# Last feed-forward of a graph network: sixteen candidates by four searches of 256 columns, exponentials by pairs of tiles

## What is computed

```
input_acts = gelu(x @ input_patterns.T)                  # 256, all of them kept
process_acts = gelu(input_repr @ process_input_weights.T)  # 1250 x 1024
top_p_acts, top_p_idx = top_k(process_acts, 128)
p_weights = softmax(top_p_acts)
agg_value = einsum('bsk,bskd->bsd', p_weights, process_values[top_p_idx])
output_acts = gelu(agg_value @ output_input_weights.T)   # 256, all of them kept
out = output_acts @ output_patterns ;  x = x + out
```

## Time and profile before

| | us |
|---|---|
| median of 3 runs | 1332.99 |
| lowest and highest | 1331.43 and 1338.83 |
| span of the profiled execution | 1331.9 |
| PE busy | 1255.2 |
| DVE busy | 557.6 |
| ACT busy | 462.4 |
| POOL busy | 198.8 |

### The profile page before, as it was taken

The page is one execution under the profiler, slowest core; times in us unless marked ns, Lnnn a source line. Parts: engine busy times, 40 slices in busy tenths (PEclk is TensorE's granted clock), DMA queues, the critical chain, the costliest instruction groups (busy, mean ns, idle before and its releaser), DMA issues.

```text
span 1331.9 us, 19378 instructions
## 1 busy us (share of the span) xinstructions
PE 1255.2 (94%) x6567; PEld 828.1 (62%) x6568; DVE 557.6 (42%) x1512; ACT 462.4 (35%) x991; POOL 198.8 (15%) x201
## 2 busy tenths in 40 slices
PE   4899999999999989989999999999989999989797
PEld 2554467466546645548877887877655587664465
DVE  8999833111124335110000000001187345677894
ACT  5799643222112220001111111111113343338893
POOL 2000000000000004711111111111173000013480
PEclk8999999999999989989999999999998999999899
DMA  9200000000020020175134611662563000200011
GB/s 206 95 1 1 1 2 1 0 1 1 0 95 21 30 108 1 20 259 207 47 118 164 233 50 46 229 231 83 205 188 117 1 33 1 72 0 0 1 30 49
DMA packets 42949, 98.25 MB, mean 74 GB/s; under 512 B 4113, under 2 KB 6603, under 8 KB 41845
## 3 DMA queue, kind: packets, MB, share of 16 engines
q1 hardware_dynamic: 28613, 68.70, 15.5%
q0 software_dynamic: 6144, 16.45, 4.5%
q10 hardware_dynamic: 8112, 12.08, 2.5%
HBM read 81.02 MB, written 16.17 MB: 73 GB/s over the span
## 4 chain that ended last, share of the span: by engine, by line
PE 73%; DVE 13%; POOL 4%; issue 4%; ACT 2%; DMA 2%; ACTq 1%; DVEq 1%; POOLq 0%
PE psum L450 34%; PE psum L1864 14%; PE psum L1908 7%; PE psum L1840 4%; PE psum L2070 4%; POOL slot_tokens L711 3%; PE psum L478 1%; PE psum L1936 1%; PE psum L1887 1%; DVE sb_hT_conv L1455 1%; ACT sb_htok L834 1%; DVE sb_stats L458 1%; DVE sb_x_res L1269 1%; PE psum L1981 1%; POOL sb_blk L655 1%
## 5 line engine op out<-in xcount | busy, mean ns | idle before, releaser
L450 PEld LDWEIGHTS psum<-sb_blk,sb_w_reg 128*128 128x128 f32 x1792 | 204.0, 192 | 12.7 <-issue 12.7
L450 PE MATMUL psum<-sb_blk,sb_w_reg 128*128 128x128 f32 x1792 | 205.2, 275 | 1.6 <-issue 1.6
L1864 PE MATMUL psum<-sb_z_reg_r,sb_hT_conv_r 125*125 125x512 f32 x400 | 169.0, 423 | 0.6 <-DVE sb_z_last L1109 0.4
L450 PE MATMUL psum<-sb_w_reg,sb_hT_conv 128*125 128x512 f32 (+1 forms) x376 | 167.2, 594 | 0.0
L1239 DVE TENSOR_TENSOR sb_blk<-sb_blk,psum 128x256 f32<-128x256 f32 x56 | 23.6, 421 | 276.9 <-ACT sb_blk L805 276.9
L1864 PE MATMUL psum<-sb_htok_r,sb_hT_conv_r 125*125 125x512 f32 x300 | 118.8, 396 | 0.0
L450 PEld LDWEIGHTS psum<-sb_w_reg,sb_hT_conv 128*125 128x125 f32 (+1 forms) x376 | 68.3, 187 | 76.6 <-issue 75.9
L450 PE MATMUL psum<-sb_hT_conv,sb_w_reg 128*128 128x416 f32 (+3 forms) x336 | 101.8, 459 | 0.8 <-ACT sb_hT_conv L484 0.8
L1908 PE MATMUL psum<-sb_w_reg,sb_blk 128*128 128x512 f32 x224 | 100.8, 592 | 0.0
L784 ACT CAST sb_hT_conv_r<-sb_a_reg 125x625 fp32r<-125x625 f32 x80 | 56.2, 716 | 115.5 <-PE psum L1864 115.5
L1864 PEld LDWEIGHTS psum<-sb_z_reg_r,sb_hT_conv_r 125*125 125x125 f32 x400 | 74.7, 187 | 23.0 <-issue 5.4
(11 more groups left out here) (396 smaller groups left out, 1753.0 us busy)
## 6 DMA issues: line engine op xcount, KB each, us to landing
sb_hT_conv<-w_expert SPq DMA_DIRECT2D x7, 2048.0 KB, 9.9
sb_w_reg<-w_expert SPq DMA_DIRECT2D x6, 2048.0 KB, 18.2
sb_hT_conv<-w_expert SPq DMA_DIRECT2D x7, 1024.0 KB, 12.4
slot_outs<-sb_blk ACTq DMA_DIRECT2D x28, 256.0 KB
sb_w_reg<-w_expert SPq DMA_DIRECT2D x6, 1024.0 KB, 20.0
sb_w_reg<-w_gnn SPq DMA_DIRECT2D x1, 4096.0 KB, 44.4
sb_w_reg<-w_qkv SPq DMA_DIRECT2D x1, 3072.0 KB, 21.3
slot_outs<-sb_blk ACTq DMA_DIRECT2D x1, 2560.0 KB, 10.6
```

What stands on the lines that cost most here:

```text
L450: ins = e.matmul(out, l, r, start=(n == 0), stop=(n == len(pairs) - 1))
L1864: ins = e.matmul(psum[0:TP, b, :], counts_at(l, 2 * i + n // NT)[:, s % HALF_T, :], z[s], start=(n == 0), stop=(n == len(pairs) - 1))
```

## The change

- `rest` is searched in four quarters of 256 columns, eight values each, into a list `found` of 32; `searched` is signalled by the last of these four instead of by the second full search, and `rest` is no longer written by DVE.
- Part 1 searches the 32 for the eight largest, copies the last value of each quarter behind them (columns 32 to 35), replaces the eight in a copy of the 32 and searches that for the next eight.
- Part 3 counts over all 36 columns of `found` instead of over the sixteen candidates, and makes the flag in two instructions instead of three.
- vec_refine's last instruction becomes a tensor_scalar with three pointers.
- The exponentials have five buffers, the two new ones in w_reg, and are made for tiles 0 and 1 together, then in each odd stage for two tiles. `len(wexp)` takes the place of 3 in the code of DVE and PE.

```
-                e.max(cand[:, i, 1:9], r).then_inc(v_own, v.up())
-                e.tensor_copy(cand[:, i, 0:1], thr[:, c]).then_inc(v_own, v.up())
+                for q in range(QUARTERS):
+                    width = N_PROC // QUARTERS
+                    e.max(found[:, q * 8:(q + 1) * 8], r[:, q * width:(q + 1) * width]).then_inc(
+                        *((searched, 1) if q == QUARTERS - 1 else (v_own, v.up())))
+                e.tensor_copy(best[:, i, 0:1], thr[:, c]).then_inc(v_own, v.up())
+                e.wait_ge(searched, i + 1)
...
-                e.match_replace(r, cand[:, i, 1:9], r, REPLACED).then_inc(v_own, v.up())
+                e.max(best[:, i, 1:9], found[:, 0:CAND]).then_inc(v_own, v.up())
+                lasts = found[:, 0:CAND].rearrange("p (q n) -> p q n", n=8)[:, :, 7]
+                e.tensor_copy(found[:, CAND:], lasts).then_inc(v_own, v.up())
                 e.wait_ge(v_own, v.n)
+                e.match_replace(others, best[:, i, 1:9], found[:, 0:CAND], REPLACED).then_inc(v_own, v.up())
+                e.wait_ge(v_own, v.n)
+                e.max(best[:, i, 9:17], others).then_inc(v_own, v.up())
...
-                e.max(cand[:, i, 9:17], r).then_inc(searched, 1)
...
-                e.tensor_scalar(cut_junk, cand[:, i, 1:17], cut[:, c], None, ALU.is_ge, ALU.add,
+                e.tensor_scalar(count_junk, found, cut[:, c], None, ALU.is_ge, ALU.add,
                                 accum_out=cut_cnt[:, c]).then_inc(v_own, v.up())
-                e.tensor_scalar(bad[:, c], cut[:, c], 0.0, None, ALU.is_le).then_inc(v_own, v.up())
                 e.wait_ge(v_own, v.n)
-                e.tensor_tensor(cut_cnt[:, c], cut_cnt[:, c], left[:, c], ALU.not_equal).then_inc(v_own, v.up())
+                e.tensor_scalar(bad[:, c], cut_cnt[:, c], left[:, c], None, ALU.not_equal).then_inc(v_own, v.up())
                 e.wait_ge(v_own, v.n)
-                e.tensor_tensor(bad[:, c], bad[:, c], cut_cnt[:, c], ALU.add).then_inc(bad_ready, 1)
+                e.tensor_scalar(bad[:, c], cut[:, c], 0.0, bad[:, c], ALU.is_le, ALU.add).then_inc(bad_ready, 1)
...
-            e.scalar_tensor_tensor(thr[:, c], left[:, c], step[:, c], thr[:, c], ALU.mult, ALU.add).then_inc(done, 1)
+            e.tensor_scalar(thr[:, c], left[:, c], step[:, c], thr[:, c], ALU.mult, ALU.add).then_inc(done, 1)
...
                 if t == NT:
                     act_exp(e, 0)
+                    act_exp(e, 1)
...
-                if t <= NT:
+                if t % 2 == 1 and t < NT:
                     act_exp(e, t - 1)
+                    act_exp(e, t)
```

More of the change, by code:

```diff
@@ L68 @@
 EARLY, EARLY_FROM, CHOICE_PARTS = 2, 5, 4
+QUARTERS = 4
 GUESS = 1.17 / (N_PROC * 0.39894)
@@ L332, in build @@
         acts = a_reg[0:TP, 0:NT * N_PROC].rearrange("p (t n) -> p t n", n=N_PROC)
-        wexp = [a_reg[0:TP, 10240:11264], a_reg[0:TP, 11264:12288], htok_flat[:, 4096:5120]]
+        wexp = [a_reg[0:TP, 10240:11264], a_reg[0:TP, 11264:12288], htok_flat[:, 4096:5120],
+                w_reg[0:TP, 1, 2064:3088], w_reg[0:TP, 1, 3088:4112]]
         rest = htok_flat[:, 0:2048].rearrange("p (r n) -> p r n", r=2)
@@ L344, in build @@
             ch[:, (2 + n) * NT:(3 + n) * NT] for n in range(11))
-        cand = ch[:, 150:150 + 17 * NT].rearrange("p (t n) -> p t n", n=17)
+        best = ch[:, 150:150 + 17 * NT].rearrange("p (t n) -> p t n", n=17)
         iota16 = ch[:, 330:346]
         cut_junk = ch[:, 350:366]
+        CAND = 8 * QUARTERS
+        cand = blk[0:TP, 440:440 + 2 * (CAND + QUARTERS)].rearrange("p (r n) -> p r n", r=2)
+        others = blk[0:TP, 520:520 + CAND]
+        count_junk = blk[0:TP, 560:560 + CAND + QUARTERS]
         bad_i = blk[0:1, 400:400 + NT].bitcast(I32)
@@ L838, in act_exp @@
             e.wait_ge(neg_ready, i + 1)
-            if i >= 3:
-                e.wait_ge(w_turned, 2 * (i - 2))
-            e.activation(wexp[i % 3], acts[:, i, :], ACT.Exp, bias=neg_max[:, i:i + 1]).then_inc(exp_ready, 1)
+            if i >= len(wexp):
+                e.wait_ge(w_turned, 2 * (i - len(wexp) + 1))
+            e.activation(wexp[i % len(wexp)], acts[:, i, :], ACT.Exp, bias=neg_max[:, i:i + 1]).then_inc(exp_ready, 1)
         def act_bad(e, i):
@@ L2332, in tensor @@
                             c = (4 * g + k) * 128
-                            ins = e.transpose(psum[:, 1 + g, k * TP:(k + 1) * TP], wexp[i % 3][:, c:c + 128],
+                            ins = e.transpose(psum[:, 1 + g, k * TP:(k + 1) * TP], wexp[i % len(wexp)][:, c:c + 128],
                                               ident[0:TP, 0:TP])
```

6 lines of the change are left out of this document (3 added, 3 removed).

## The result

| | before | after |
|---|---|---|
| median, us | 1333.37 | 1373.69 |
| lowest and highest, us | 1331.43 and 1338.83 | 1372.34 and 1377.48 |
| runs | 4 | 4 |
| span of the profiled execution, us | 1331.9 | 1370.6 |

The changed kernel takes 1.0305 times the time before (95% interval 1.0285 to 1.0326). The predicted time was 1372.5 us, the range 1366 to 1384.

What follows compares the result with a forecast made beforehand. DVE's chain of waits was taken to bound the last feed-forward, at 7.50 us a stage. Fallback 42.0, part 2 -2.7 and part 3 +0.2 gave +39.5 on the median of 1332.99: 1372.5 us, range 1366 to 1384.

Steps and rivals of the forecast that it cites:

- The fallback: Weighing of tile 2: token 321 sets the flag, so the whole tile takes sixteen uncovered search-and-replace rounds; +42.0 us, chance 0.86.
- Part 2: First loop: refinements no longer held under POOL's second pass, so ACT idles less; -2.7 us, bounds -1.5 and -2.9.
- ACT's three idles: First loop: waits of 0.39, 1.15 and 1.31 us; first two go (1.54), 1.2 of the third behind tile 0's cut.
- Part 3: Second loop: cut held by POOL's second pass, stages about 8.0 us in tiles 4 to 7, others shorter; +0.2, bounds -3 and +4.
- PE's restart: Behind the fallback: PE restarts at half its clock after some 40 us idle, losing about 2.7 us of work, partly hidden.
- No fallback: Rival, tile 2: token 321's flag comes out zero; -5.5 to +0.6 us, likeliest 1330.5; chance 0.07.
- Long hold: Rival, second loop: POOL's first pass too holds the weighing to its end; stages of 9.0 in four tiles, 1376.5 us; chance 0.04.
- Second tile: Rival, weighing: a second tile also falls back, 42 us more, 1414 us; chance 0.03.
- A rule against a row: DVE against POOL's first pass: skill page says exclusion for the whole instruction; a row shows release about 1.1 us in.

Runs made afterwards that it cites:

- x3_refine: The kernel before with only the refinement's second instruction changed, to one tensor and two pointers as sources; 1332.91 us, ratio 0.9994 to before.
- x11_searches: x1_blocks64 with refinements in their old form and exponentials one at a time in three buffers; 1332.19 us in one run.
- x1_blocks64: The changed kernel with each of the four searches over 256 columns taken as four blocks of 64; 1332.11 us, ratio 0.9990 to before.
- x10: x7 without the load of the flag and without the other branch, every tile weighed with its cut; 1326.32 us in one run.
- x7: x1_blocks64 with POOL let go by the last search over 32 instead of the fourth over 256; 1328.03 us, ratio 0.9951 to before.
- x6: x1_blocks64 with the weighing of the tile before moved straight behind the four searches; 1329.65 us, ratio 0.9971 to before.

## Why the prediction was right

**The fallback.** Named by token, tile and number of rounds, and found so. That the whole branch had to be priced, though it had never run, decided the case: 42.0 predicted, 42.61 measured. The search and replace rows (1.22, 1.21, 0.09) hold in the branch to 0.01. The error is the drain: 0.08 us against the 0.03 to 0.04 of the gaps, under the 0.18 that bounded it; 42.0 was a choice between 41.4 and 46. PE and ACT stood empty for 44 to 45 us, not for 38.

**Part 2, -2.7.** The last GELU of the first loop ends 49.42 us behind the memset before and 46.79 after (1240.29 - 1190.87 and 1235.25 - 1188.46). Timelines of ACT before and after, its end:

```profile
1240.09 0.20 ACT L1075 ACTIVATION_READ_ACCUMULATOR sb_a_reg<-psum 125x1 f32 x1
```
```profile
1235.05 0.20 ACT L1082 ACTIVATION_READ_ACCUMULATOR sb_a_reg<-psum 125x1 f32 x1
```

That is -2.63. No L1341 is above 0.27, the cut of tile 0 starts at 1229.68, 0.04 behind POOL's pass, and is not held; of ACT's three idles, 0.46 us are left. Up to tile 1's weighing -2.27 remain, the rest going into a filler that took 8.35 us for 8.00 (from the GELU's end to tile 0's transposes). But the name of the term was wrong: at the GELU's end x3_refine, the refinements alone, has -1.31, and x11_searches, the searches alone, -1.25. The first two idles go with the refinements, the third with the searches. As the prediction says, it goes because POOL's pass over tile 2 is released by tile 0's count; but in x3 that pass still waits for the second search (L1347), and only the searches' early signal takes this wait away.

**Part 3, +0.2.** From tile 1's weighing on, without the fallback's rounds: -1.61 + 2.88 - 0.50 = +0.77. The mechanism was right in the four stages in which POOL still works: the cut is held under the second pass. Stages of 8.0 were forecast, and they take 8.00, 8.22, 8.17 and 8.22, 0.6 in all. The term mis-sized is the weighing's distance from the last search's start, 1.2 in the sum, 1.22, 1.45, 1.40 and 1.44 in the trace; a later weighing delays POOL's second pass (2.14 us at the first of them, 2.30 to 2.35 at the others), and the cut ends with that pass. The hold stood in the sum at 1.8 and came at 1.5. But that the whole came out at +0.8 beside +0.2 is in part luck. Stages 2, 3, 8 and 9 were to be 1 to 2 us shorter; from search to search stage 2 is 1.8 shorter, stage 3 not at all (without the block), stage 8 only 0.1, and from the search of tile 9 to its weighing it is 0.6 longer. Against that stood PE's restart, up to 2.7 us of lost work, which cost nothing. The prediction took the whole at +0.2 without adding these pieces up. That the four-column copy can be held was named too: 0.15 in stages 4 to 7, but 1.58 in tile 3, ahead of the fallback. Timelines of DVE and POOL, after:

```profile
1254.07 1.58 DVE L1359 COPY sb_blk<-sb_blk 125x4 f32<-125x4 f32 x1
```
```profile
1253.47 2.15 POOL L774 TENSOR_TENSOR sb_htok<-sb_hT_conv,sb_a_reg 125x1024 f32<-125x1024 bf16 x1
```

**The cold restart** is there (1.93, 3.52 at half clock) and x1_blocks64, without it, is no shorter than after less its block: no cost shown, where up to 2.7 us were thought possible.

**The sum.** 39.5 was forecast for the part that changed and 41.11 came. The profiled spans differ by only 38.7, because the untouched part happened to be 2.41 us shorter; the medians differ by 40.3. That 1372.5 lies so near 1373.69 owes a little to that: block, part 2 and part 3 each came 0.4 to 0.6 us dearer than forecast.

**The rivals.** No fallback: was put at 1330.5, within -5.5 to +0.6; x1_blocks64, which is this case made, gave 1332.11, a ratio of 0.9990. Long hold: out, since in the stage above the weighing starts at 1313.44 with 0.86 us of POOL's first pass to go, and takes its 1.28. Second tile: did not occur.

**A rule against a row, once more.** All holds by POOL's second pass in the traces shown here last until its end (1.58, 1.73, 1.88, 2.12 us). Those by the first pass end early, 1.14 us behind its start in the earlier trace rows (1247.59 to 1248.73) and 1.15 at the cut of tile 2 in after (1250.54 to 1251.37 + 0.32). In x10 the cut, of 0.72 us, ends at 1285.59. The pass was itself 0.85 late behind the weighing, so it can be put at 1284.44, and that is 1.15 again. The Trainium skill, page "SBUF — State Buffer", section "Who interferes with whom", has whoever issues first keep the shared ports for its whole instruction. The trace agrees for the second pass, and for the weighing that makes the first pass 3.69 in x10. It does not for the first pass as the holder.

## What to carry to other kernels

A cheap path with a test for when it fails must be priced by how often the test fires on the real data, by the largest group that one failure drags along, and by the slow path's full length, even when no trace has ever shown that path. Whether it fires is in the data, and can be counted before anything runs. How data is divided over lists decides that as much as the list's size: 256 columns in four blocks of 64 never failed here, 256 in a row failed once and lost 42 us. When a shortened instruction stream does not shorten its stage, look at which instruction now starts under another engine's hold: here a signal moved by 0.9 us was worth more than all three parts of the change together.

## What the runs showed of the hardware that I had not expected

- A drain between two dependent DVE instructions leaves a gap of 0.08 us, a semaphore 0.03 to 0.04.
- DVE is idle for 0.7 to 1.3 us from a short instruction to one behind a loaded flag and a branch (L1398 at tiles 2 to 7 in after, x1 and x7; 0.60 to L1390), and not at all at tiles 5 and 7 of x6, where 1.4 us of searches were issued ahead of it.
- A copy of four columns with one source is held under POOL's second pass (1.58 in after), while a tensor_scalar of one column with pointers never was (0.27 in all first-loop rows of after).
- POOL's first pass takes 2.84 alone, and 3.69 to 3.92 where a DVE instruction with two sources over 1024 columns runs at its start (before, x10).
- An instruction of DVE and a pass of POOL that start within 0.05 us of each other went either way: the cut was held for 2.21 us in x11 and passed in 0.24 in x1.
